# First cross attention: a pair's weight transposes issued directly behind the next pair's scores

## The reference, cut to what matters

```
ctx = layer_norm(context, g1, b1)          # 375 rows
lat = layer_norm(x, g2, b2)                # 112 rows
q = lat @ Wq
k, v = split(concat([ctx, lat]) @ Wkv)     # 487 keys
w = softmax(mask(q_head . k_head * scale)) # 112 x 487 for each head
out = concat over heads(w @ v_head) @ Wout
x = x + out
```

## Time and profile before

| What | Value |
|---|---|
| Time, median of 3 runs | 1812.6 us (1812.02 to 1827.2) |
| Profiled execution | 1835.7 us, span 1833.9 us |
| First cross attention, from the first batch's first scores to the last batch's output projection | about 233 to 1090 us of the span |
| One middle batch | 52.6 us |
| Share of the span that TensorE has a matmul, weight load | 93%, 73% |
| DVE, ACT, POOL busy | 55%, 40%, 36% |

### The profile page before, as it was taken

One profiled execution on the slowest core, in us unless ns is written; L12 is line 12 of the kernel. 1 busy time (PEld: TensorE's weight loads), 2 busy tenths in 40 slices (PEclk: granted clock), 3 DMA queues, 4 the chain that ended last, 5 costly groups with the idle time before them and its releaser, 6 DMA issues. The chain is left out here.

```text
span 1833.9 us, 32673 instructions
## 1 busy us (share of the span) xinstructions
PE 1697.7 (93%) x11198; PEld 1338.0 (73%) x11198; DVE 1003.3 (55%) x2462; ACT 742.6 (40%) x2109; POOL 661.4 (36%) x575
## 2 busy tenths in 40 slices
PE   7899899999999999999999976999998799986898
PEld 6687677777777777777777765989877677654566
DVE  5466466665556666655556532242255388764664
ACT  2255344444444444544444420333203477641210
POOL 1022245555454555554555523233420133361000
PEclk9999999999999999999999967999998899996999
DMA  3100300000000000000000015565210000010000
GB/s 96 55 1 1 120 1 10 10 10 9 9 5 4 9 9 9 9 9 9 1 8 9 1 48 179 163 233 184 90 43 20 1 1 1 2 56 1 1 21 20
DMA packets 48805, 67.40 MB, mean 37 GB/s; under 512 B 11827, under 2 KB 42771, under 8 KB 46035
## 3 DMA queue, kind: packets, MB, share of 16 engines
q1 hardware_dynamic: 47186, 62.66, 11.1%
q0 software_dynamic: 1536, 3.67, 0.7%
HBM read 57.02 MB, written 9.31 MB: 36 GB/s over the span
## 5 line engine op out<-in xcount | busy, mean ns | idle before, releaser
L667 POOL TENSOR_SCALAR l0x_p<-l0x_p,l0x_inv 112x488 f32<-112x488 f32 x256 | 387.1, 1524 | 377.6 <-DVE l0x_inv L761 377.6
L870 ACT ACTIVATE l0x_p<-l0x_s,l0x_low 112x488 f32<-112x488 f32 x256 | 178.3, 697 | 292.7 <-DVE l0x_low L750 292.7
L750 DVE CUSTOM_DVE_ANT_0 l0x_s<-l0x_score_ps,l0x_bias 112x488 f32<-112x488 f32 x256 | 160.2, 664 | 135.3 <-PE l0x_score_ps L1010 117.1
L737 DVE TENSOR_TENSOR l0x_kT_lo<-l0x_proj_ps,l0x_kT_hi 128x488 fp32r<-128x488 f32 x128 | 85.3, 666 | 107.4 <-ACT l0x_kT_hi L860 107.4
L1018 PE MATMUL l0x_pT_ps<-ident,l0x_p 112*122 112x112 f32 x1024 | 126.2, 264 | 14.9 <-POOL l0x_p L667 14.9
L1018 PEld LDWEIGHTS l0x_pT_ps<-ident,l0x_p 112*122 112x122 f32 x1024 | 109.3, 140 | 36.4 <-POOL l0x_p L667 23.0
L1031 PEld LDWEIGHTS l0x_oT_ps<-l0x_pT,l0x_v 122*64 122x64 f32 x2048 | 102.4, 139 | 43.3 <-issue 33.1
L1031 PE MATMUL l0x_oT_ps<-l0x_pT,l0x_v 122*64 122x112 f32 x2048 | 130.0, 270 | 3.9 <-DVE l0x_pT L756 3.1
L1883 POOL TENSOR_TENSOR l1a_pn<-l1a_p,l1a_inv 112x896 f32<-112x896 f32 x32 | 53.9, 1684 | 197.5 <-DVE l1a_inv L1912 197.5
L966 PE MATMUL l0x_proj_ps<-l0x_kvT_hi,l0x_wkv_hi 128*128 128x488 f32 x256 | 111.0, 434 | 2.9 <-DVE l0x_kvT_lo L725 2.9
L1968 ACT ACTIVATE l1a_p<-l1a_p,l1a_shift 112x112 f32<-112x112 f32 x256 | 95.4, 375 | 32.0 <-DVE l1a_shift L1906 32.0
(11 more groups left out here) (354 smaller groups left out, 3705.1 us busy)
## 6 DMA issues: line engine op xcount, KB each, us to landing
l0f_w<-in_l0f_w SPq DMA_DIRECT2D x21, 1024.0 KB
l0x_c_in<-in_ctx SPq DMA_DIRECT2D x16, 375.0 KB
l0f_context<-in_ctx SPq DMA_DIRECT2D x16, 375.0 KB
sorted_x<-l0x_zeros SPq DMA_DIRECT2D x1, 2816.0 KB, 15.4
l0f_xs<-sorted_x SPq DMA_DIRECT2D x21, 128.0 KB, 2.2
sorted_y<-l0f_ys SPq DMA_DIRECT2D x21, 128.0 KB, 1.7
l0x_wkv<-in_l0x_wkv SPq DMA_DIRECT2D x2, 1024.0 KB, 9.6
x<-in_x SPq DMA_DIRECT2D x4, 448.0 KB, 8.3
```

Source lines behind the costliest of these rows:

```text
L667: nc.gpsimd.tensor_scalar(p[:, i % 2, a, :], p[:, i % 2, a, :], inv[:, i % 2, a:a + 1], None, ALU.mult).then_inc(pn_ready, 1)
L750: nc.vector.tensor_tensor_reduce(s_sb[:, h % 2, :], score_ps[0:S, h % 2, 0:KEYS], bias[:], -SCALE, 3.4e38, ALU.add, ALU.min, low[:, h:h + ...
L870: nc.scalar.activation(p[:, h // 2 % 2, h % 2, :], s_sb[:, h % 2, :], ACT.Exp, scale=-1.0, bias=low[:, h:h + 1], accum_out=total[:, h:h + ...
```

## The change

In the first cross attention, in each slot that had a projection between the scores and the transposes, `transpose_p` now stands ahead of it, directly behind the scores. In slot 0 it changes places with the second half of the query projection; in slots 1, 2 and 4 to 7 with one value or key projection, in the last batch with a piece of `route`. Slot 3 is as it was. Nothing is added or removed, and no wait is changed; the other engines' instructions and their order are the same.

```diff
                 for i in range(HP):
                     score(b, i)
                     if i == 0:
-                        project_q(b, 1)
                         if not first:
                             transpose_p(b - 1, HP - 1)
+                        project_q(b, 1)
                         project_high_v(b, 0)
                         if not first:
                             weigh_values(b - 1, HP - 1)
                         continue
+                    transpose_p(b, i - 1)
                     if i <= 2:
                         project_high_v(b, 2 * i - 1)
                     elif i >= 4 and not last:
                         project_k(b + 1, 2 * i - 8)
                     elif i >= 4:
                         route(2 * i - 8)
-                    transpose_p(b, i - 1)
                     if i == 1:
```

## The result

The changed kernel takes 1890.95 us (median of four runs, 1888.72 to 1893.57), against 1819.86 us for the kernel before on the same chip (four runs, 1812.02 to 1827.2). The ratio is 1.039, with a 95% interval of 1.033 to 1.045: slower by 71 us. The forecast was 1882 in a range of 1843 to 1910, so it held, and its mechanism is what the trace shows. The four times of the kernel before fall in two groups, 1812.02 and 1812.6, 1827.12 and 1827.2, and the median lies between them, so the 71 us are no surer than the interval says: 60 to 82.

What follows compares the result with a forecast made beforehand. TensorE's in-order queue was taken as the bound: 14 middle batches at 4.23 us (59), first batch 3.5, last 6, together +69 on 1812.6, giving 1882 us; 8-in-10 range 1843 to 1910, the forecast's own 1855 to 1900.

Steps and rivals of the forecast that it cites:

- switching: Slots 1, 2 and 4 to 7: two projections now touch, the first matmul takes 0.39 not 0.47 us, -0.08 each.
- The three effects: In the moved slots: POOL's ready time against the transposes' earlier need, that ready time itself moving later, and less switching.
- The ready time: POOL's end for a pair, from its score start: 7.27 to 7.92 us before; needed at slot length plus 1.20.
- The shifts: Later ready times, as projections and the copies ahead of the softmax chain come later: +0.70, +0.50 or +0.65 us by pair.
- Slot 0's weighing: Slot 0: waits 0.35 us for ACT's pT copy, which comes 0.70 later; with the transposes' 0.37 stall, +0.72.
- The stalls in slots 1 and 2: Transposes waiting for POOL's weights: 1.21 and 1.46 us; less 0.08 each, +1.13 and +1.38 us a batch.
- The stall given to slot 3: Slot 3, order unchanged: transposes wait 1.63 us for POOL against 1.05 before, +0.58 us a batch.
- The ends: First batch about +3.5 us, without slot 0's transposes; last batch +6, between 4 and 9, with 2.4 of router waits.
- Half of it: Rival: ready times don't move, so only the lost cover costs, 1.4 us a batch, +23 us, 1836 us; chance 11%.
- The clock falls: Rival: stalls in slots 1 to 3 halve TensorE's clock once a batch, 53 us on top, 1935 us; chance 6%.
- TensorE makes up for the stalls: Rival: gaps in array time absorb the waits, only switching is left, -8 us, 1805 (or 1788) us; chance 7%.

Runs made afterwards that it cites:

- the chain forward: Changed kernel with DVE's transposes copy and inversion directly behind the masks, ACT's exponentials ahead of the key or query copy; 1808.6 us, 0.994 of the kernel before.
- the two runs of the chain: Changed kernel with DVE and ACT reordered (the chain forward), 1808.6 us, 0.994; and with DVE's reordering alone, ACT as before, 1831.5 us, 1.004.
- the mended kernel: To the chain forward, slot 3's output projection split around the transposes and, in step 3, DVE's inversion ahead of the copy; 1798.2 us, 0.988 of the kernel before.

## Why the prediction was right, and where its terms were off

**The bound.** TensorE's queue sets the pace: every stall at its head lengthened the period by its own size. The new waits read from the trace are 0.42, 1.06 and 1.35 us in slots 0 to 2 (the last with the first head's 0.22), 0.37 in slots 5 and 6, and 0.52 and 0.56 for the two weighings; less some 0.4 of switching that is 4.2, and the period grew by 4.25. The predicted 4.23 is nearer to it than its terms are: slots 0 and 2 came out 0.20 and 0.42 longer than forecast and slot 3 0.59 shorter, and these cancel. So close a hit is partly luck; the forecast's own range, 1855 to 1900, says better how sure it was.

**The three effects.** The ready time counted from the pair's score start, with the two copies queued ahead, was the step that separated +69 from +23 us. It is shown by bringing the chain forward: without a change to TensorE's order, 5.1 us a period come back. The shifts themselves came as put down: +0.70 for pair 0, +0.50 for pairs 1 and 2 and +0.65 for pairs 4 to 7 were forecast, and 0.69, 0.46, 0.46 and 0.71 measured. That the pieces in front are to blame, on both engines, is shown by the two runs of the chain; the prediction gave slots 4 to 7 to ACT's copy alone and left out DVE's piece. The saving from projections of one kind that touch was put at 0.08; slots 4 and 7, which have no stall, show 0.06 to 0.07.

**Slot by slot.** Forecast and measured lengths, slots 0 to 7: 6.63 and 6.83; 6.65 and 6.57; 6.45 and 6.87; 7.74 and 7.15; 6.71 and 6.73; 7.07 and 7.10; 8.88 and 8.88; 6.71 and 6.74. Three slots were off by more than a tenth of a us.
- Slot 0's weighing waits 0.52, not 0.35. DVE's copy releases it, not ACT's: it stands behind the split of the queries and ends at 635.01 + 0.61 = 635.62, 0.07 us after ACT's, and the weighing starts 0.15 us after that where a lag of 0.05 was reckoned.
- The stalls in slots 1 and 2 were given as 1.21 and 1.46 and are 1.06 and 1.35. Slot 0 got 0.20 us longer than forecast, and what one slot waits more, the next one waits less.
- The stall given to slot 3 (1.63 against 1.05) didn't come. The prediction said that a wait of slot 2's weighing would only move part of it there, and so it was: 0.56 of waiting in slot 2, and slots 2 and 3 together are 14.02 where 14.19 was forecast.

**The ends.** For the first batch 3.5 was forecast and 2.25 measured, for the last 6 and 4.5. In the last batch the router's second pieces do wait for ACT's copy, as forecast, three times 0.63 instead of 0.8:

```profile
1122.92 1.22 PE L1054 MATMUL l0x_proj_ps<-l0f_wr,l0x_x1T 128*112 128x8 f32 x8 [0.63 <-ACT l0x_x1T L850]
```

In the first batch the rest is the clock. Slot 4, in which TensorE waits for nobody in either trace, takes 8.90 us before and 7.32 after, and the granted clock was at the lower level (0.5, 1.2 GHz) for 4.7 us of it before and for 1.3 after. Without that slot the batch got 3.8 us longer, where 3.5 was forecast. In the last batch the clock was low for about as long in both traces, 32 and 34 us. Its slots 0 to 3 got 3.49 longer, where 3.81 was forecast; the other 1.0 us stands against a forecast of 2.4. The three new waits are in it, and a saving that was not foreseen: in the kernel before, the last pair's transposes, at the end of this batch, waited 0.65 and 0.82 us for POOL, and now they don't. How much of the difference each of the two makes is left open.

**The total.** The stage cost 66.3 us where 69 was forecast. The medians differ by 71 us. The predicted 1882 is 9 us under the measured 1891, and 7.3 of that is the reference: 1812.6 was the median of three runs, 1819.86 that of four. That 69 lies so near to 71 says less than it seems, since the 71 could be 60 to 82.

**The rivals.** *Half of it* needed ready times that don't move; they moved by 1.1 to 1.8 us with the stalls in them, and by 0.5 to 0.7 without. *The clock falls* is out for the middle batches: 1.00 with three stalls close together. *TensorE makes up for the stalls* is out: the weight loads' share was 77% before, and 78% in the mended kernel, in which no gap shows on TensorE. So the rule of the Trainium skill, "Perfetto Trace Analysis", section Identifying the Most-Contended Engine, to judge TensorE's headroom by the share of weight loads, doesn't hold for this stream of matmuls (the page names MFU, the share of the peak arithmetic, beside it, which was not worked out here): it would have given a time near 1813, and 1891 was measured. Here the matmuls' busy share was the better guide, 98% with 2% to be had, and the best kernel took them.

## What to carry to other kernels

Before a consumer is moved up in an in-order queue, count its producer's ready time from the event that starts the chain, and ask what in the chain's own queues stands behind work that the move delays: the loop through the delayed projection made this change three times as dear (4.25 us a batch) as the lost cover alone was worked out to be (1.4). An order of one engine is good or bad only together with the orders of the others; the same TensorE order was 3.9% slower with the softmax chain behind the projections' copies and 0.6% faster with it in front. And two cures priced alone have to be priced again together: look for what the second delays that the first has put in front.

## What the runs showed of the hardware

POOL's pair of multiplications takes longer when certain DVE work runs beside it. In most steps it takes 2.99 us, also where DVE's L718 and L742, which read PSUM, run beside it; in slot 1, where DVE normalises the context (L709), 3.27; in the kernel with the chain forward, where DVE's L725 runs with two inputs from SBUF, 3.71; and 3.87 where that and the update of x (L78 to L83) follow each other. POOL's row, chain forward, slot 3:

```profile
614.39 3.71 POOL L667 TENSOR_SCALAR l0x_p<-l0x_p,l0x_inv 112x488 f32<-112x488 f32 x2 [2.12 <-DVE l0x_inv L761]
```

DVE's own L725 took 1.22 us for its two instructions there, no more than elsewhere, so here POOL paid. DVE can pay too: in the same kernel its L711, beside POOL's pair 1 (3.09 us), takes 0.75 us, where it takes 0.40 in the kernel before.

```profile
605.45 0.75 DVE L711 TENSOR_SCALAR l0x_lat<-x,mv,rstd 112x256 f32 x1
```

The Trainium skill, page "SBUF — State Buffer", section SBUF: two separate sides, says that DVE with two SBUF inputs and GpSimd share a port pair that one of them holds for a whole instruction while the other is blocked. For L725 the trace agrees in kind, with 0.7 us lost beside 1.2 us of such work; what each instruction held is not to be seen in it.

A granted clock of 1.00 (2.4 GHz) survived three stalls of 0.8 to 0.9 us idle within 20 us, batch after batch, with TensorE 93% busy.
